# A convolution and local-attention kernel: w1T loaded in three transfers, one subtraction on another engine, two steps moved

## The reference, cut to what matters

```python
# x: (16, 32, 32, 128), NHWC; C = 128
perceived = depthwise_3x3(x, w_perc) + b_perc               # 3C channels, 3 per input channel
hid = gelu(einsum('bphw,dp->bdhw', perceived, w_up1) + b_up1)   # 2C channels
dx  = einsum('bdhw,cd->bchw', hid, w_up2) + b_up2
h   = x + dx
q, k, v = split(einsum('bhwc,dc->bhwd', h, w_qkv) + b_qkv)
scores = 9 dot products of q with the zero-padded 3x3 neighbourhood of k, / sqrt(C)
out = h + sum_i softmax(scores)[i] * v_shifted[i]
```

## Time and profile before

| | us |
|---|---|
| median of 3 runs (394.73 to 394.92) | 394.77 |
| profiled execution, whole | 394.93 |
| its span, first to last instruction | 393.1 |

### The profile page before, as it was taken

The page is one execution under the profiler, slowest core; times in us unless marked ns, Lnnn a source line. Parts: engine busy times, 40 slices in busy tenths (PEclk is TensorE's granted clock), DMA queues, the critical chain, the costliest instruction groups (busy, mean ns, idle before and its releaser), DMA issues.

```text
span 393.1 us, 10470 instructions
## 1 busy us (share of the span) xinstructions
PE 382.4 (97%) x3664; PEld 359.6 (91%) x3664; DVE 340.3 (87%) x919; ACT 256.5 (65%) x542; POOL 180.0 (46%) x159
## 2 busy tenths in 40 slices
PE   5999999999999999999999999999999999999995
PEld 4999998999989999999999999999999999999874
DVE  4999999999988889888888988888898888887795
ACT  6645478929485774848477484847748484773893
POOL 5784563646445262635525263552526355132111
PEclk9999999999999999999999999999999999999999
DMA  7420301434151513325150332515033231403003
GB/s 226 183 67 3 121 2 25 139 45 170 31 187 20 171 32 65 141 39 173 25 181 14 74 131 39 173 26 175 21 71 132 39 107 26 121 12 85 3 27 135
DMA packets 56313, 33.98 MB, mean 86 GB/s; under 512 B 47200, under 2 KB 48096, under 8 KB 56288
## 3 DMA queue, kind: packets, MB, share of 16 engines
q1 hardware_dynamic: 56000, 33.61, 30.3%
q10 hardware_dynamic: 288, 0.05, 0.1%
HBM read 19.86 MB, written 8.39 MB: 72 GB/s over the span
## 4 chain that ended last, share of the span: by engine, by line
PE 83%; DVE 11%; issue 2%; DMA 1%; ACT 1%; POOL 0%; DVEq 0%; ACTq 0%
PE m_ps L484 45%; PE work L539 10%; PE s_ps L609 9%; PE work L583 7%; PE s_ps L592 6%; PE s_ps L578 2%; PE s_ps L575 2%; PE s_ps L576 2%; DVE t L970 1%; DMA wp<-w_perc 1%; DVE tlo L977 1%; DVE h_around L1238 1%; DVE h_lo L987 1%; DVE s_ps L1012 1%; PE work L562 1%
## 5 line engine op out<-in xcount | busy, mean ns | idle before, releaser
L484 PE MATMUL m_ps<-thi,whi 128*128 128x256 f32 x558 | 158.9, 285 | 0.9 <-DVE ru_sb L1058 0.8
L484 PE MATMUL m_ps<-thi,wlo 128*128 128x256 f32 x558 | 155.5, 279 | 0.0
L484 PE MATMUL m_ps<-tlo,whi 128*128 128x256 f32 x558 | 154.3, 276 | 0.0
L484 PEld LDWEIGHTS m_ps<-thi,whi 128*128 128x128 f32 x558 | 104.8, 188 | 4.3 <-issue 1.0
L484 PEld LDWEIGHTS m_ps<-tlo,whi 128*128 128x128 f32 x558 | 105.6, 189 | 0.6
L484 PEld LDWEIGHTS m_ps<-thi,wlo 128*128 128x128 f32 x558 | 104.9, 188 | 0.0
L1404 POOL TENSOR_TENSOR hid_lo<-hid,hid_hi 128x1024 fp32r<-128x1024 f32 x30 | 72.2, 2406 | 27.9 <-ACT hid_hi L741 21.4
L1381 POOL TENSOR_TENSOR fc<-xp 128x512 f32<-128x512 f32 x16 | 21.3, 1333 | 98.3 <-DVE tlo L977 91.8
L731 ACT ACTIVATE hid<-y,b1eff 128x1024 f32<-128x1024 f32 x31 | 35.7, 1152 | 33.1 <-DVE y L1081 23.1
L715 ACT CAST thi<-t 128x1024 fp32r<-128x1024 f32 (+1 forms) x32 | 25.1, 832 | 48.6 <-DVE t L970 48.5
L807 ACT ACTIVATE p_sb<-p_sb,negmax 128x101 f32<-128x101 f32 x128 | 46.8, 369 | 6.2 <-DVE negmax L1111 6.1
(11 more groups left out here) (156 smaller groups left out, 765.6 us busy)
## 6 DMA issues: line engine op xcount, KB each, us to landing
xp<-x_planes SPq DMA_DIRECT2D x16, 640.0 KB, 5.3
xr<-x_rows SPq DMA_DIRECT2D x16, 512.0 KB, 4.1
out<-o_sb SPq DMA_DIRECT2D x28, 256.0 KB, 4.0
pt<-ptc SPq DMA_DIRECT2D x140, 32.0 KB, 1.9
pt<-ptc SPq DMA_DIRECT2D x28, 28.0 KB, 1.9
out<-y SPq DMA_DIRECT2D x3, 256.0 KB, 2.5
w1T<-w SPq DMA_DIRECT2D x1, 384.0 KB, 3.6
out<-y SPq DMA_DIRECT2D x2, 128.0 KB, 2.4
```

The lines of the kernel that those rows point to most:

```text
L484: last = pe.matmul(bank[:, col + first:col + end], a[:, j, dy, half * P:(half + 1) * P], c[:, par, T_PLACE[j], first + by:end + by], start ...
```

## The change

1. `w1T` is loaded by three transfers of 128 KB (one per m), each with a semaphore of its own. Image 0's planes go to ScalarE's queue, third on it. TensorE starts on the first third with six instead of five `keep_busy` matmuls and waits for the others ahead of `middle_tap`; VectorE waits for the second and the last third ahead of the operations that use them.
2. GpSimd's `differences(2, 0)` waits for `y_part_done` 4, the four parts of `y` of image 0's first half.
3. `low_hid(0, 1)` leaves GpSimd. VectorE does the subtraction (`low_hid_first`) between `combine_y(1, 0)` and `transform_ab(2, 0)`, with the semaphore `hlo_dve_done`, for which TensorE's `up(1)` and ScalarE's `gelu(1, 1)` now wait. `low_hid(0, 0)` adds 2 to `hlo_done`, so that later counts hold.
4. In VectorE's `last()` the second `turn_p` stands between the copies of row 2 and of row 3 of tiles 0 to 3, and `add_h(n, 1, 1)` behind the copies of tiles 4 to 7.

```diff
-            sp.dma_start(w1T[:, :, :].rearrange("p m d -> p (m d)"), w1_c).then_inc(first_in, 16)
-            load_planes(0, 0)
+            for m in range(3):
+                sp.dma_start(w1T[:, m, :], w1_c[:, m * HID:(m + 1) * HID]).then_inc(w1_in[m], 16)
...
-                pe.wait_ge(first_in, 16)
-                keep_busy(5)
+                pe.wait_ge(w1_in[0], 16)
+                keep_busy(6)
+                for m in (1, 2):
+                    pe.wait_ge(w1_in[m], 16)
...
+                if is_image(n, 1):
+                    pe.wait_ge(hlo_dve_done, 1)
+                else:
+                    pe.wait_ge(hlo_done, n * 2)
...
+            act.dma_start(xp[:, 0, :, :, :].rearrange("p k r w -> p (k r w)"), x_planes[0]).then_inc(x_loaded[0], 16)
...
+            def low_hid_first():
+                dve.wait_ge(hhi_done, 2)
+                nc.vector.tensor_tensor(hid_lo[:, 1, :], hid[:, 1, :], hid_hi[:, 1, :].bitcast(F32),
+                                        ALU.subtract).then_inc(hlo_dve_done, 1)
...
+                    dve.wait_ge(w1_in[m], 16)
...
-                for row in (2, 3):
-                    place(1, row, range(0, 4))
+                place(1, 2, range(0, 4))
                 turn_p(n, 1)
-                add_h(n, 1, 1)
+                place(1, 3, range(0, 4))
                 dve.wait_ge(ptc_done, n * 2)
                 place(1, 2, range(4, 8))
+                add_h(n, 1, 1)
...
                 if is_image(n, 0):
                     sums_ab(1)
+                    pool.wait_ge(y_part_done, 4)
                     differences(2, 0)
                     pool.wait_ge(y_part_done, 8)
                     low_hid(0, 0)
                     return
                 if is_image(n, 1):
-                    low_hid(0, 1)
                     sums_ab(2)
```

More of the change, by code:

```diff
@@ L195, in build @@
         TAPS = (0, 2)
-        first_in = sem("first_in")
+        w1_in = [sem(f"w1_in{m}") for m in range(3)]
         filters_in = sem("filters_in")
@@ L264, in build @@
         hlo_done = sem("hlo_done")
+        hlo_dve_done = sem("hlo_dve_done")
         h_hi_done = sem("h_hi_done")
@@ L555, in up @@
                     add(c, w2lo, 1, hid_hi, start=False, stop=False)
-                pe.wait_ge(hlo_done, n * 2)
+                if is_image(n, 1):
+                    pe.wait_ge(hlo_dve_done, 1)
+                else:
+                    pe.wait_ge(hlo_done, n * 2)
                 for c in range(NCH):
@@ L727, in gelu @@
                     act.wait_ge(b1_done, 1)
-                if from_image(n, 1):
+                if is_image(n, 1) and half:
+                    act.wait_ge(hlo_dve_done, 1)
+                elif from_image(n, 1):
                     act.wait_ge(hlo_done, n * 2 + (half - 1))
@@ L759, in _ @@
             nc.scalar.activation(primer[:, :], h_around[:, 0, 0:1], ACT.Gelu).then_inc(primed, 1)
-            act.wait_ge(first_in, 16)
+            act.wait_ge(w1_in[0], 16)
             act.wait_ge(filters_done, 1)
@@ L947, in _ @@
             dve.wait_ge(filters_done, 1)
-            dve.wait_ge(first_in, 16)
             def rows(a):
@@ L1265, in body @@
                     combine_y(1, 0)
+                    low_hid_first()
                     transform_ab(2, 0)
@@ L1404, in low_hid @@
                 nc.gpsimd.tensor_tensor(hid_lo[:, half, :], hid[:, half, :], hid_hi[:, half, :].bitcast(F32),
-                                        ALU.subtract).then_inc(hlo_done, 1)
+                                        ALU.subtract).then_inc(hlo_done, 2 if is_image(n, 0) else 1)
             def normalise(n, g):
```

## The result

The changed kernel takes **396.17 us** (median of 15 executions, 395.03 to 397.99) against 394.77 for the kernel before (15 executions, 394.42 to 395.10) beside it on the same chip. The ratio is 1.0042, with a 95% interval of 1.0028 to 1.0057: slower by 0.42%, where 0.3% faster was forecast. (The ratio takes in the whole spread; the medians are 1.40 us, or 0.35%, apart.) As telling as the median is the width: 0.7 us before, 3.0 us after. The profiled execution of the changed kernel took 395.06, nearly its best. A second profiled execution of the same kernel (experiment 7) took 397.38, and both are needed.

A forecast was written before the change was run, and what follows sets the result against it. TensorE, busy nearly all the time, was taken as the bound, losing only to VectorE's waits and a late first product. 0.81 (differences) + 0.45 (start) + 0 + 0 = 1.26 us off 394.77 gave 393.5, range 392.8 to 394.2.

The forecast's parts named there:

- The start: Split w1T, moved planes and an extra keep_busy matmul make TensorE's first product 0.45 us earlier.
- The row-by-row pattern: Transfers on two queues alternate row by row, so a small one ends with the big one beside it.
- near 6.1: Landing of w1T's last third, with the planes; VectorE's chain would then come 0.5 us earlier.
- The bound given, 6.6: Latest landing allowed for w1T's last third; VectorE's chain would then gain 0.
- Rival (d): Start: last third lands d us after 6.62, gain 0.81 - d, slower by 0.2% from d = 1.6; chance 0.04.
- the Trainium skill's rule on whole packets: A DMA engine takes a whole packet from one ring before the next; by it VectorE's shift would be 0.9 us.
- both chains meet at 16.81: TensorE's preparation and VectorE's chain both end at the first product, so the later one sets its gain.
- the two cases: TensorE's start gains 0.15 us if the clock rises when it did, about 0.65 if it rises as much earlier.
- The differences: GpSimd's later differences of image 2 remove both TensorE waits for VectorE up to 34.42: 0.81 us gained.
- The 0.3 at image 2: Possible loss of 0 to 0.3 us at image 2's first product, waiting for `tlo`; put into the range only.
- The second low half: Subtraction moved to VectorE makes it 1 us earlier afterwards, but TensorE has no wait there: price 0.
- The tail: Last turn of P between copies: SyncE's last stores start as before, price 0, bounds +0.3 and -0.5.

The follow-up runs named there:

- experiment 7: The changed kernel unaltered, profiled a second time: 397.38 us.
- experiment 1: Changed kernel with its start put back (w1T in one transfer, planes behind it on SyncE's queue, five keep_busy matmuls): 394.11 us, ratio 0.9981.
- experiment 9: Kernel before with only the tail changed (last turn of P ahead of VectorE's second row of copies): 394.57 us, ratio 0.9994.
- 8: Kernel before with only GpSimd's differences of image 2 made later: 394.25 us, ratio 0.9986.
- experiment 2: Kernel before with the changed start alone: 396.67 us, ratio 1.0049.
- experiment 5: Kernel before with one keep_busy matmul and two of the three last warming matmuls left out: 395.99 us, ratio 1.0040.
- experiment 4: Changed kernel with image 0's planes back on SyncE's queue, behind the three thirds of w1T: 395.05 us, ratio 1.0012.
- experiment 6: Changed kernel with nine keep_busy matmuls for six: 395.53 us, ratio 1.0019.
- experiment 3: Changed kernel with seven warming matmuls for three ahead of TensorE's first product: 395.79 us, ratio 1.0034.
- experiment 11: Changed kernel with w1T in two transfers, planes behind them on SyncE's queue, seven keep_busy matmuls: 394.90 us, ratio 1.0000.
- experiment 12: Changed kernel with six more keep_busy matmuls, two by two between the small ones ahead of TensorE's first product: 395.24 us, ratio 1.0012.

## Why the prediction was wrong

**The start, -0.45 forecast, about +2.1 measured.** Three steps of it failed.

*Where the last third lands.* The row-by-row pattern was the right one: the third landed with the planes (VectorE uses it at 6.93 and GpSimd has the planes at 7.2 in the profiled execution). The time "near 6.1" was wrong. It was that of the planes in the kernel before, kept although they now start third on another queue; GpSimd gets them at 7.2 to 8.1 in the six traces that have them there, and VectorE gets the last third at 6.9 to 7.8. Why they are later there than behind w1T was not settled. The bound given, 6.6, was no bound. The first product follows VectorE's first operation on the last third by 10.3 in all six, so the landing goes straight to TensorE. Rival (d) was this mechanism, with 0.04 for a landing more than 1.6 after 6.62; its d was 0.3 and 1.1 in the two traces. By its own sum, 0.81 - d, that is 394.3 to 395.1, and not yet the result. Part of what is missing is the base: 6.62 was the latest of the six traces with the old start (6.02 to 6.62), so against their median, 6.19, the d of the two is 0.7 and 1.5.

By the Trainium skill's rule on whole packets ("DMA: Bandwidth & Descriptors", section "Queues, rings and completion order") VectorE would, by the prediction's working, have been 0.9 earlier; the 1.22 us of wait speak against it once more, as `ident_bf` had.

*What an earlier TensorE does.* That both chains meet at 16.81 and the later one counts was applied to the time alone. The earlier chain was TensorE's, and the extra matmul was read as work to be timed, not as cover: no sentence asked what TensorE does between its own end and VectorE's. The pace rose between 6.1 and 9.6 in the thirteen new traces, 3.1 to 6.0 us after TensorE's start, against 10.2 in the earlier trace rows, so the preparation ends up to 1.9 us earlier than in the one trace I had, and the gap opens. That both chains met there was itself a chance of that execution, as the gaps of 0.76 in experiments 1 and 9 show. The sum of this term is off as well: with its own paces (0.43 and 0.22) the two cases give 0.08 and 0.56, not 0.15 and 0.65. The 0.45 chosen lies within either pair.

*The clock after a gap.* It wasn't priced at all. The profile of before showed no fall, but it showed both levels, and a stretch at the lower one costs up to half its length. A rival of that kind could have been written, though its length, 3.4 us, and so the 1.7, no row gave. The measured price is 1.5 where the waits are gone. The Trainium skill ("TensorE: Matmul & The Clock Gate", section "HAM oscillation — how this bites in real kernels") warns that gaps lower TensorE's clock, though of longer ones than the 1.95, 1.97 and 2.06 us that were followed by a fall here. Its Part 1, cited in the prediction for the moment of the rise, is borne out: that moment differed from execution to execution, and so did whether there was a fall.

**The differences, 0.81 forecast, 0.5 measured.** Right in mechanism: `tlo` 1.83, the `y` part 0.42, both waits gone, `ru_sb` in time. The 0.3 at image 2 was named and put into the range; it belonged into the sum, since `tlo` ended just ahead of that product and everything ahead of it moved.

**The second low half, 0 forecast.** 0 beside the differences, 0.39 slower alone. The prediction asked what is queued behind the subtraction; it didn't ask what VectorE releases earlier on GpSimd.

**The tail, 0 forecast, 0 to 0.2 gained.** Right within what can be measured, but not exact in mechanism. In the changed kernel `L1230` starts at 386.81, the very moment of the earlier trace rows, and SyncE's last issues follow without a gap. The equality is a coincidence: VectorE's transpose ahead of the copies starts 0.16 earlier than before (382.00 for 382.16), so the row of stores has lost that much, and the first three issues have won 0.20 (1.60 for 1.80), which the prediction had named as a bound.

```profile
388.05 1.60 SPq L400 DMA_DIRECT2D out<-y  x3
389.69 0.95 SPq L405 DMA_DIRECT2D out<-y  x2
```

Without the start term the prediction's sum is 394.0; without the start the chip gave 394.11. That is partly luck: 0.81 was forecast for the differences alone, and 0.46 (8), 0.18 (9) and the play between the sets make up the 0.69.

## What to carry to other kernels

Matmuls that only keep TensorE busy are cover for what follows: whoever makes TensorE's preparation earlier, or what it waits for later, has to fill what opens; here filling between the tiny matmuls left no fall in 11 executions. When one transfer is split so that part of it is early, ask beside what the last part now lies and when that lands, and give it as a bound the latest landing of its new neighbour, not the old one. And read the spread of the executions with the median: a width that grows fourfold suggests a cause that comes and goes, and one trace of the best execution will not show it. Nor is one trace a base: the start of the kernel before varied by 0.6 us between traces, and the prediction worked from the latest one.

## What the runs showed of the hardware

- The granted clock fell after TensorE's gaps of 1.95, 1.97 and 2.06 us, not in them: 0.7 to 1.2 us after TensorE had resumed at full load, and for 3.4 us each time (2 x 1.70 in the stretches of experiment 7). The three traces with a fall are those of experiments 2, 5 and 7; a gap of 2.06 in the profiled execution of the changed kernel had none, nor had gaps of 1.51 and 1.39 in those of experiments 4 and 6.
- A transfer of 128 KB with 1 KB rows, beside one of 640 KB with 5 KB rows on the other queue, landed only shortly before that did (used from 6.9 to 7.8 us, the other from 7.2 to 8.1, six traces), where the same transfer with that one behind it on its own queue landed by 4.3 (experiment 4).
- Three issues of SyncE for one (0.75 to 2.09, against 0.75 to 1.15) and planes behind them that GpSimd got at 8.1 (experiment 4, one trace) instead of 5.8 to 6.6 (six traces): more than the 0.9 us of later issue; why more was not settled.
- VectorE's operation for `wg` took 0.18 us when it started at 3.9 or later, and 0.48 to 0.60 when it started at 3.1 to 3.2 beside GpSimd's `MEMSET` of `pt` (1.02 to 3.68): it ended at 3.71 each time (traces of the changed kernel and of experiments 2, 3, 4, 6, 7, 11 and 12).
